# Graph attention with layer norm: Q rows read from a table in DRAM, and a one-hot made from distance features

## What is computed

```python
Qh = (h @ WQ).reshape(N, H, D)          # the same for K and V
Eh = (edge_attr @ WE).reshape(-1, H, D)
score = einsum('ehd,ehd,ehd->eh', Kh[src], Qh[dst], Eh) / sqrt(D)
score = exp(clip(score, -5.0, 5.0))
wV = segment_sum(Vh[src] * score[:, :, None], dst)
Z = segment_sum(score, dst)
x = layernorm(x + wV / (Z + 1e-6))
```

## Time and profile before

| | |
|---|---|
| median of three runs | 2109.49 us (2108.01 to 2111.33) |
| the profiled execution | 2111.6 us, its span 2109.8 us |
| TensorE matmul | 1560.1 us busy, 74% of the span |
| VectorE | 1487.4 us, 70% |
| ScalarE | 1317.4 us, 62% |
| GpSimd (POOL) | 1558.1 us, 74% |
| DMA | 342.89 MB, 163 GB/s on average |
| first gather, last gather (start) | 47.3 us, 2086.7 us |

### The profile page before, as it was taken

How to read it: one execution, slowest core, us unless ns; L and a number is a source line. 1 busy time by engine, 2 the same in 40 slices (tenths; PEclk the granted TensorE clock), 3 DMA queues, 4 the chain that set the end, 5 groups by cost and what they waited for, 6 DMA issues and landing times.

```text
span 2109.8 us, 49493 instructions
## 1 busy us (share of the span) xinstructions
PE 1560.1 (74%) x14786; PEld 1436.8 (68%) x14787; DVE 1487.4 (70%) x3785; ACT 1317.4 (62%) x3270; POOL 1558.1 (74%) x1628
## 2 busy tenths in 40 slices
PE   8678777777777777777776777777777777777775
PEld 6577777677667666767666766666666667676674
DVE  4777677667767767767776776776777777677666
ACT  2667666666656666666666666666666666666663
POOL 2777777777777777777777777777777777777774
PEclk9899999989999999999999999999999999999998
DMA  7965555555555555555555555555555555555552
GB/s 236 272 176 165 161 162 161 156 158 160 154 164 157 159 162 156 161 159 158 162 159 159 157 159 160 160 161 160 157 163 158 158 162 152 162 161 159 160 156 82
DMA packets 217419, 342.89 MB, mean 163 GB/s; under 512 B 86480, under 2 KB 112056, under 8 KB 217163
## 3 DMA queue, kind: packets, MB, share of 16 engines
q0 software_dynamic: 77376, 211.39, 34.8%
q1 hardware_dynamic: 139211, 128.05, 21.6%
q10 hardware_dynamic: 576, 0.26, 0.0%
HBM read 325.24 MB, written 9.60 MB: 159 GB/s over the span
## 4 chain that ended last, share of the span: by engine, by line
POOL 40%; issue 20%; DVE 11%; PE 11%; DMA 8%; ACT 5%; DVEq 4%; SPq 1%; POOLq 0%
POOL kv L444 40%; DMA kv<-kv_table,src_idx 7%; PE psW L588 4%; DVE msg L938 3%; ACT hot L721 3%; DVEq L247 3%; DVE acc L955 3%; PE psE L554 2%; PE psQ L577 2%; DVE prod L921 2%; ACT hot L726 2%; PE psH L564 2%; DVE score L926 1%; DVEq L955 1%; PE psE L507 1%
## 5 line engine op out<-in xcount | busy, mean ns | idle before, releaser
L444 POOL DMA_INDIRECT kv<-kv_table,src_idx x1612 | 1549.6, 961 | 513.3 <-issue 495.7
L916 DVE TENSOR_TENSOR prod<-kv,psE 128x512 f32<-128x512 f32 x403 | 276.5, 686 | 472.9 <-DMA kv<-kv_table,src_idx 284.5
L588 PE MATMUL psW<-msg,hot 128*128 128x136 f32 x3224 | 473.6, 290 | 111.3 <-DVE msg L938 111.1
L564 PE MATMUL psH<-ident,hot 128*128 128x128 f32 x1612 | 264.8, 288 | 332.3 <-ACT hot L726 327.2
L721 ACT ACTIVATE hot<-iota,local 128x128 f32 x1612 | 508.8, 386 | 2.0 <-issue 1.5
L588 PEld LDWEIGHTS psW<-msg,hot 128*128 128x128 f32 x3224 | 406.5, 192 | 132.2 <-DVE msg L938 130.9
L564 PEld LDWEIGHTS psH<-ident,hot 128*128 128x128 f32 x1612 | 175.0, 142 | 411.3 <-ACT hot L726 410.6
L554 PE MATMUL psE<-w_e,attrT 128*128 128x128 f32 x3224 | 432.1, 278 | 0.0
L748 ACT ACTIVATE msg<-clipped 128x32 f32<-128x32 f32 x403 | 92.3, 229 | 522.4 <-DVE clipped L932 515.1
L554 PEld LDWEIGHTS psE<-w_e,attrT 128*128 128x128 f32 x3224 | 398.1, 194 | 0.0
L577 PE MATMUL psQ<-Qp,hotT 128*128 x4836 | 340.1, 221 | 8.9 <-DMA Qp<-Qp 8.9
(11 more groups left out here) (94 smaller groups left out, 352.7 us busy)
## 6 DMA issues: line engine op xcount, KB each, us to landing
attr<-in_edge_attr_dram SPq DMA_DIRECT2D x403, 256.0 KB
kv<-kv_table,src_idx POOLq DMA_INDIRECT x1612
kv_table<-kv SPq DMA_DIRECT2D x12, 512.0 KB, 4.0
Qp<-Qp SPq DMA_DIRECT2D x23, 192.0 KB
hot<-in_x_dram SPq DMA_DIRECT2D x12, 256.0 KB, 4.7
xT<-in_x_dram SPq DMA_DIRECT2D x8, 384.0 KB
out_dram<-xT SPq DMA_DIRECT2D x45, 64.0 KB
src_idx<-in_src_dram SPq DMA_DIRECT2D x50, 16.0 KB
```

Of the source, the lines that this page charges most:

```text
L444: nc.gpsimd.indirect_dma_start(out=kv[:, u, t, :], out_offset=None, in_=kv_table, in_offset=bass.IndirectOffsetOnAxis(ap=src_idx[:, b % 2, ...
L564: last = nc.tensor.transpose(psH[:, t * P:(t + 1) * P], hot[:, g % HOTS, t, :], ident[:, :])
L588: last = nc.tensor.matmul(psW[:, u % 2, 0:MW], hot[:, g % HOTS, t, :], msg[:, g % MSGS, t, :], start=(t == 0), stop=(t == TILES - 1))
```

## The change

**Q.** The three bf16 parts are no longer kept on the chip. They are stored to `q_table` in DRAM, three rows of 256 B for a node, through a staging ring of 3 chunks: the first part of chunk c waits until the store of chunk c-3 has landed. For every group SyncE loads 128 consecutive rows (42 nodes by 3 parts, 32 KB) from the node of its first edge on (`load_near_q`, ring of 4); the row number is read into a register (`load_bases`, 8 at a time). The 12 selecting matmuls become 4. `move_q` is gone.

**The one-hot for Q.** Its turned form is no longer got by turning the other one. With d the distance of an edge's node from the first node of the group, row 3j+k of it is relu(1 - (j - d)^2) = relu(2jd - d^2 + 1 - j^2). A matmul of 3 by 512 gives 2jd - d^2 from the features d, and d^2 in two bf16 parts; ScalarE adds 1 - j^2 and takes the relu while it copies. The features are made in the head (VectorE and ScalarE), stored to `near_table` in DRAM (1.57 MB), and loaded for four groups at a time.

**The head.** K and V go through their own staging ring of 4 chunks; ScalarE copies every second pair. SyncE issues the loads of indices (three of them) behind the store of chunk 9, and the four loads of attributes behind the store of chunk 10, that is ahead of the stores of chunks 11 and 12. VectorE clears `acc` (GpSimd did).

**Rings.** `RINGS` is 16, so a gather waits for the messages of group g-16. All indices have room at once, so their loads wait for no gather. The one-hots have 4 buffers and not 5, and ScalarE makes that of group g+2, not g+3. TensorE and ScalarE read no registers any more.

```diff
-RINGS = 8
-HOTS = 5
+TURN = 8
+RINGS = 16
+NEAR = 42
+PARTS = 3
+QROWS = 4
+FEATS = 4
+KV_STAGES = 4
+Q_STAGES = 3
+HOTS = 4
@@ SyncE
+            def load_near_q(g, base):
+                if g >= QROWS:
+                    sp.wait_ge(q_sel, g - QROWS + 1)
+                sp.dma_start(q_near[:, g % QROWS, :], q_rows[bass.ds(base, P), :]).then_inc(q_in[g % QROWS], 16)
+            def load_feats(k):
+                if k >= 2:
+                    sp.wait_ge(feat_mm, (k - 1) * FEATS)
+                sp.dma_start(feats[:, k % 2, :, :], near_table[k * FEATS:(k + 1) * FEATS, :, :]
+                             .rearrange("g f e -> f g e")).then_inc(feats_in[k % 2], 16)
-            load_indices(0)
-            load_indices(1)
-            for u in range(ATTRS):
-                load_attr(0, u)
...
+                if c == CH - 4:
+                    for b in range(3):
+                        load_indices(b)
+                elif c == CH - 3:
+                    for g in range(ATTRS):
+                        load_attr(g)
+            sp.wait_ge(feat_lo, 1)
+            sp.dma_start(near_table.rearrange("(c p) f e -> p c f e", p=P), feat_rows).then_inc(near_stored, 16)
...
+                if c < CH - 1:
+                    sp.dma_start(q_table[w0 * P:(w0 + n) * P, :].rearrange("(w p) f -> p w f", p=P),
+                                 q_stage[:, c % Q_STAGES, 0:n, :, :].rearrange("p w k d -> p w (k d)"))\
+                        .then_inc(q_stored[c % Q_STAGES], 16)
...
@@ GpSimd
-                if past(g, RINGS):
+                if g >= RINGS:
                     pool.wait_ge(msg_ok, g - RINGS + 1)
+                if g == RINGS - 5:
+                    pool.wait_ge(near_stored, 16)
@@ TensorE
+            def near_products(g):
+                if g % FEATS == 0:
+                    pe.wait_ge(feats_in[g // FEATS % 2], (g // FEATS // 2 + 1) * 16)
+                if g >= 1:
+                    pe.wait_ge(hotT_ok, g)
+                nc.tensor.matmul(psF[:, :], coef[:, :], feats[:, g // FEATS % 2, g % FEATS, :], start=True, stop=True)\
+                    .then_inc(feat_mm, 1)
...
-                    for part in range(3):
-                        last = nc.tensor.matmul(psQ[:, u % 2, t * P:(t + 1) * P], hotT[:, u % 2, t * P:(t + 1) * P],
-                                                Qp[:, bass.ds(slot, 1), part, :].rearrange("p a d -> p (a d)"),
-                                                start=(part == 0), stop=(part == 2))
+                    last = nc.tensor.matmul(psQ[:, g % 2, t * P:(t + 1) * P], hotT[:, g % 2, t * P:(t + 1) * P],
+                                            q_near[:, g % QROWS, :], start=True, stop=True)
...
+            def step(g):
+                if g + 2 < G:
+                    turn_attr(g + 2)
+                    near_products(g + 2)
+                if g + 1 < G:
+                    edge_products(g + 1)
+                    select_q(g + 1)
+                if g >= 1:
+                    sum_messages(g - 1)
@@ ScalarE, in the head after each copy of x; and for each group
+                if c >= 1:
+                    copy_kv(c - 1)
+                if CH - 8 <= c < CH - 4:
+                    near_features(c - (CH - 8))
+                elif c >= CH - 4:
+                    square_high(c - (CH - 4))
...
+                nc.scalar.activation(hotT[:, g % 2, :], psF[:, :], ACT.Relu, bias=near_bias[:, 0:1]).then_inc(hotT_ok, 1)
@@ VectorE, in the head after the copy of chunk c
+                if c == 1:
+                    find_bases()
+                elif c == 2:
+                    find_main(0)
+                elif c == 3:
+                    find_main(1)
+                elif c == 4:
+                    keep_main()
+                elif c == 5:
+                    find_places(0)
+                elif c == 6:
+                    find_places(1)
+                elif c == 7:
+                    keep_places()
+                elif c == 8:
                     place_groups()
```

More of the change, by code:

```diff
@@ L358, in _ @@
                     .then_inc(x_res_in, 16)
-            for b in range(2, LAG + 2):
+            for b in range(3, LAG + 2):
                 load_turn(b)
@@ L450, in _ @@
[L450 to L456 removed]
+                        out=kv[:, g % RINGS, t, :], out_offset=None, in_=kv_table,
+                        in_offset=bass.IndirectOffsetOnAxis(ap=src_idx[:, g, t:t + 1], axis=0))\
+                        .then_inc(kv_in[g % RINGS], 16)
@@ L459, in _ @@
+            for i in range(KV_STAGES):
+                pool.wait_ge(kv_stored[i], 16 * len(range(i, CH, KV_STAGES)))
+            for g in range(G):
+                gather(g)
             pool.wait_ge(table_ok, 1)
@@ L632, in _ @@
+            select_q(0)
+            for g in range(G):
+                step(g)
+            sum_messages(G - 1)
             pe.wait_ge(table_ok, 1)
@@ L862, in _, with find_main @@
-            for pair in range(-(-WIN // 2)):
-                copy_kv(pair)
-                if pair == 7:
-                    place_first_edges()
-                elif pair == 11:
+            def find_main(half):
+                dve.wait_ge(prep, 3 + half)
+                if half == 0:
+                    nc.vector.tensor_scalar(main, near, 0.0, None, ALU.is_ge).then_inc(prep, 1)
+                else:
+                    nc.vector.scalar_tensor_tensor(main, near, float(NEAR - 1), main, ALU.is_le, ALU.mult)\
+                        .then_inc(prep, 1)
@@ new lines, in keep_main, with find_places @@
+            def keep_main():
+                dve.wait_ge(prep, 5)
+                nc.vector.scalar_tensor_tensor(near, near, 1.0, main, ALU.add, ALU.mult).then_inc(near_ok, 1)
+            def find_places(half):
+                if half == 0:
+                    nc.vector.tensor_scalar(dst_rows, dst_rows, P - 1, None, ALU.bitwise_and).then_inc(prep, 1)
+                else:
+                    dve.wait_ge(prep, 6)
+                    nc.vector.tensor_scalar(local_rows, dst_rows, 1.0, None, ALU.add).then_inc(prep, 1)
@@ new lines, in square_low @@
+            def square_low(c):
+                dve.wait_ge(feat_hi, c + 1)
+                last = nc.vector.tensor_tensor(feat_rows[:, c, 2, :], square[:, c, :], feat_rows[:, c, 1, :],
+                                               ALU.subtract)
+                if c == GC - 1:
+                    last.then_inc(feat_lo, 1)
+            for c in range(CH):
+                copy_kv(c)
+                if c == 1:
[13 more added lines that the diff above has]
+                elif c == 8:
@@ L867, in _ @@
                     place_groups()
+            for c in range(GC):
+                square_low(c)
             dve.wait_ge(turned, 2)
@@ L954, in add_sums @@
                     where = acc[half, bass.ds(w, 1), :].rearrange("p a m -> p (a m)")
-                    last = nc.vector.tensor_tensor(where, psW[half, u % 2, 0:MW], where, ALU.add)
+                    last = nc.vector.tensor_tensor(where, psW[half, g % 2, 0:MW], where, ALU.add)
                 last.then_inc(added, 1)
@@ L1039, in _ @@
+            windows = load_windows(B_LAST * TURN - 2, G - B_LAST * TURN + 2)
+            for g in range(B_LAST * TURN, G):
+                step(g, windows[g - B_LAST * TURN])
+            messages(G - 1)
+            add_sums(G - 2, windows[-2])
+            add_sums(G - 1, windows[-1])
             dve.wait_ge(added, G)
```

665 lines of the change are left out of this document (305 added, 360 removed).

## The result

| | before | after |
|---|---|---|
| median, same chip | 2110.41 us (2108.01 to 2116.67) | 2134.38 us (2132.77 to 2135.89) |
| profiled execution, its span | 2111.6, 2109.8 us | 2132.77, 2131.0 us |
| first gather, last gather (start) | 47.3, 2086.7 us | 50.5, 2107.6 us |
| distance, step | 2039.4, 1.2659 us | 2057.1, 1.2769 us |

The change makes the kernel slower: the ratio is 1.0109, with a 95% interval of 1.0085 to 1.0132. Between the two profiled executions lie 21.2 us: 3.2 ahead of the first gather, 17.7 between first and last, 0.3 behind. The forecast was 2112.4 us in a range to 2122. The first gather came where it was forecast, and the pace of the gathers was off.

A forecast was written before the change was run, and what follows sets the result against it. GpSimd's chain of gather issues was taken as the bound. 2111.6 + 0.2 + 3.2 - 0.5 + 0 + 0 gave 2114.5 us; the profiled run stood 2.1 above the median, hence 2112.4 us, range 2103 to 2122.

The forecast's parts named there:

- The bound: Whole kernel: GpSimd's chain of gather issues sets the time, 1.266 us a step, and POOL never pauses.
- (1): TensorE before the first gather: 4.7 us gained, VectorE's new steps cost 4.9 us, ScalarE's mostly hidden; sum +0.2 us.
- (2): SyncE's DMA queue before the first gather: attribute loads ahead of the last two K and V stores cost +3.2 us.
- (3): Ring of K and V, 16 groups for 8: one gather's wait for a full ring goes, -0.5 us; 16 is necessary.
- (4): Pace of the gathers between first and last: unchanged, 0 us, from -10 to +10.
- (5): Work behind the last gather: nothing changes, 0 us, from -2 to +1.
- The clock: TensorE over the kernel: about 1190 us busy, with its clock over 0.9.
- The rival: TensorE idles more and drops to the lower clock; a third of the groups slower, 107 us, 2220 us; chance 0.04.

## Why the prediction was wrong, point by point

**The bound** was right. After the first gather POOL waits for nobody, 23.4 us lie behind the last gather for 23.1, and the length of the gathers (with the one pause of the ring of 8) accounts for the pace in every kernel where the chip was not the slow one.

**(1) TensorE in the head:** forecast +0.2 us, measured +0.7, since K and V end at 38.41 + 2.65 = 41.06 us for 40.33. The timelines of after, VectorE, then TensorE, then ScalarE:

```profile
15.01 1.22 DVE L867 TENSOR_SCALAR acc<-acc 128x2048 f32<-128x2048 f32 x1
16.98 2.28 DVE L869 SCALAR_TENSOR_TENSOR acc<-acc 128x2048 f32<-128x2048 f32 x1
...
24.87 1.99 PE L553 MATMUL psE<-w_kv,xT 128*128 128x256 f32 x8 [2.46 <-ACT xT L684]
...
28.00 1.99 PE L553 MATMUL psE<-w_kv,xT 128*128 128x256 f32 x8 [0.70 <-ACT xT L684]
...
28.31 1.13 ACT L708 ACTIVATE kv<-acc 128x512 bf16<-128x512 f32 x1
29.32 1.25 ACT L709 ACTIVATE kv<-acc,minus_one 128x512 f32<-128x512 f32 x1
...
34.55 0.65 ACT L714 ACTIVATE kv<-kv 128x512 bf16<-128x512 f32 x1
```

VectorE's new steps take 1.22 and 2.28 us, where 1.2 and 2.3 were worked out, and the wait for x before 17 us is gone. But from 24.87 us on TensorE waits for ScalarE: its two feature steps take 1.13 and 1.25 us where two of about 0.60 were reckoned (these two read every fourth element, and the later L714 over as many columns, read in order, took 0.65; that the order is the reason was not tried), and a chunk takes it 3.1 us for the 2.5 forecast. So the length of VectorE's steps was right, but not what they cost: of the 4.9 us put down for them TensorE waited 0.21 us for VectorE. It waited 2.46 + 0.70 + 0.68 + 0.70 = 4.5 us for ScalarE, which the prediction had hidden behind VectorE (and ScalarE's first feature step had itself waited 2.10 us for VectorE's L874). That the sum came out within half a microsecond is luck.

**(2) The DMA queue:** forecast +3.2 us, measured 3.2 - 0.7 = +2.5. The queue of SyncE and two stretches of after (busy by engine, clock, DMA share, GB/s), against the earlier trace rows:

```profile
37.36 2.48 SPq L286 DMA_DIRECT2D src_idx<-in_src_dram  x3
...
40.52 2.47 SPq L295 DMA_DIRECT2D attr<-in_edge_attr_dram  x4
...
43.51 0.36 SPq L333 DMA_DIRECT2D kv_table<-kv_stage  x1
```

```profile
43.00:47.00 4.00, 2.96 (x24) 2.38 (x22) 1.84 (x4) 2.39 (x6) 0.00 (x0) 1.00 1.00 345
...
326.00:2087.00 1761.00, 1299.00 (x8625) 1080.91 (x8625) 1235.55 (x3237) 1108.89 (x2761) 1340.23 (x1381) 0.86 0.59 164
```

After the last store was issued the queue still ran at 345 GB/s for 4 us: the attributes are paid for there, as forecast, and the kernel with the loads early shows it by experiment. The first gather comes at 50.54 us:

```profile
50.54 1.11 POOL L492 DMA_INDIRECT kv<-kv_table,src_idx  x1 [17.72 <-DMA kv_table<-kv_stage]
```

Over the runs on all chips but the slow one it scatters, 50.0 to 52.0 us with the changed head and 45.6 to 50.0 with the old one, so the fit to a tenth is luck. The means, 51.0 and 47.5, are 3.5 us apart, where 3.4 was forecast.

**(3) The ring** was right in what makes it necessary: VectorE's first product runs at 96.50 us (98 forecast), and a ring of 8 pauses at gather 33. But the gain of 0.5 us rests on a misread row. The gather of 1.46 us in the earlier trace rows did not wait for a full ring. It is a collision too, 0.04 us behind the start of the messages on VectorE (timeline of before), and it ends 1.50 us after it:

```profile
87.95 0.68 DVE L938 TENSOR_TENSOR msg<-kv,msg 128x512 f32<-128x512 f32 x1
```

A full ring shows as idle time ahead of a gather, as the 10.57 us above, and not as a longer gather. So this row belonged to (4), with the other end of the sawtooth, and the 0.5 us had no ground.

**(4) The pace of the gathers** is the step that failed. It stood at 0 with 10 us to either side, and measured +17.7. The collision with L938 was named, and so was the row, though the phase that was said to matter was that of L926, and it is that of L938. The failure is in its size, in two moves of the working. First, "the trace has 24, so most of them miss" took the share of hits of before for a property of the kernel; it was one outcome of a phase, and a better one than an even spread. Second, the bounds were a third of that outcome. From the earlier trace rows they could have been had: a gather 0.15 us behind is held by 0.41, so if the hold ends at a fixed time the window is some 0.5 us wide, and evenly spread phases give 0.5/1.27 x 403 x 0.25 = 40 us, plus the 2.5 that stay without any collision: 17 above the 25.6 of before; and with no hits at all, 23 below. The runs reach from -23 (extra 2.5) to +33 (59.1), so even this is a middle and not an upper end. The cause I had given for a shift, 403 more loads, was wrong as well. Taking the loads out left the slow pace, putting as many into the kernel before left the good one; another order on TensorE and a delay on VectorE broke it.

**(5) The end:** 0 forecast, +0.3 measured.

**The clock.** TensorE was to be busy 1190 us with a clock over 0.9. It was busy 1566.3 at 0.86, with 4442 fewer matmuls: the sums take 331 ns each for 290, and idle time turned into longer matmuls. The forecast of this was wrong. The rival had the lower clock right and its price of 107 us wrong: between 326 and 2087 us TensorE was busy 74% in both kernels, and with the collisions gone the pace was 1.252 us at a clock of 0.87 and of 0.99 alike.

**What stays open:** by which path TensorE's order moves the phase between VectorE and POOL, and whether it would cost anything once the collision is gone.

## What to carry to other kernels

Where an engine that issues gathers is the bound, look at the mean and the median of its instructions: a mean above an unchanged median is a collision, and its price is a matter of phase. Bound it from below by no hits at all, take an even spread as the middle, and leave room above it (the worst run here lay 17 us beyond), whatever the trace happens to show. Then take the collision away, not the phase: one operand in PSUM made both kernels 1.1 to 1.2% faster than the kernel before here, as much as the whole change had cost. And while such a collision stands, a reordering on an engine that is far from the bound isn't free.

## What the runs showed of the hardware

A gather's issue (0.947 us) is held by a 128x512 product with two operands in SBUF only if it starts 0.04 to 0.56 us behind it, and then ends 1.50 us after that product's start. I had expected contention to stretch whatever it overlaps.

On one chip the same kernel before took 2942 us and the changed one 2854.45, ratio 0.9706 (0.9685 to 0.9727): the sign turns. What the changed kernel waited for there (total us, times, longest), and two rows of its TensorE in the head:

```profile
PE psW L626 <- issue: 902.1, 260, 7.0
ACT attrT L763 <- remote: 707.1, 194, 5.0
POOL kv L492 <- DVE msg L986: 690.2, 210, 34.2
```

```profile
87.37 2.08 PE L562 MATMUL psW<-w_q,xT 128*128 128x128 f32 x8 [14.05 <-issue]
109.07 2.08 PE L562 MATMUL psW<-w_q,xT 128*128 128x128 f32 x8 [19.62 <-issue]
```

TensorE was idle for more than 3 us at a time 161 times there, 793 us in all, for 50 times and 215 us on the chip of the result. It stood still for 14 and 20 us in the head, waiting for nothing that the profile shows, and the other engines wait for it. The gathers aren't the bound there. The changed kernel has 38,997 instructions for 49,493, but the number alone doesn't make it the faster one: with the exponential in PSUM it has 39,400 and took 2940.22 us. The cause is open. There the two that lengthen collisions elsewhere, the ring of 8 and the turn moved, were faster than their counterparts too (0.9632 and 0.9949).
